# Shift's transfers issued by ACT, SP's loads and spills in another order, and every band applied by DVE

## The reference, cut to what matters

```
y = x + attention(layernorm(x)) @ W_proj + b_proj
out = y + moe(layernorm(y))

attention, per head (window m = 64, p = 8, four levels):
  A0[q] = q . k of the 64 keys that end at the query           (a band of 64 in a window of 128 keys)
  Al[q] = q . 8 pooled keys of the previous block, l = 1..4     (blocks of 64, 128, 256, 512 rows)
  mn = min over the five levels of max(A_level)
  weights = exp(A - mn), pooled ones times 8, 16, 32, 64; divided by their sum
  output = weights . values (and pooled values)

moe: 8 experts, softmax gate, the top 2 renormalised; expert e: (a * sigmoid(b)) @ Wo + bo, a and b the halves of y @ W1[e] + b1[e]
```

## Time and profile before

| | |
|---|---|
| runs | 333.83, 325.39, 331.42 us; median 331.42 |
| profiled execution | 322.26 us, of which the span of its instructions is 320.4 us |
| PE busy | 272.8 us, 85% of the span |
| DVE, ACT, POOL busy | 189.8, 159.8, 129.0 us |
| start, until unit 0's first score | 0 to 41.3 us |
| attention, eight units | 41.3 to 205.9 us |
| experts | 205.9 to 320.4 us |
| transfers | 28.35 MB |

### The profile page before, as it was taken

How to read it: one execution, slowest core, us unless ns; L and a number is a source line. 1 busy time by engine, 2 the same in 40 slices (tenths; PEclk the granted TensorE clock), 3 DMA queues, 4 the chain that set the end, 5 groups by cost and what they waited for, 6 DMA issues and landing times.

```text
span 320.4 us, 6664 instructions
## 1 busy us (share of the span) xinstructions
PE 272.8 (85%) x2382; PEld 225.5 (70%) x2382; DVE 189.8 (59%) x515; ACT 159.8 (50%) x325; POOL 129.0 (40%) x217
## 2 busy tenths in 40 slices
PE   7784588499798599937999796799999999999994
PEld 5563486487686589826787685577888877888883
DVE  7837428528436243520465638776787698777773
ACT  7574235135346336722429437464458654555551
POOL 7103203402000000110016238167788478888882
PEclk9796956859779579995989996999999999999999
DMA  8139843340569533145117355010000000000000
GB/s 219 29 119 332 283 112 74 92 93 1 170 255 267 130 74 110 21 102 154 28 30 231 77 186 177 5 27 8 8 11 9 9 10 8 18 10 8 16 10 16
DMA packets 25391, 28.35 MB, mean 88 GB/s; under 512 B 12976, under 2 KB 19248, under 8 KB 25360
## 3 DMA queue, kind: packets, MB, share of 16 engines
q1 hardware_dynamic: 25216, 27.55, 29.5%
q10 hardware_dynamic: 144, 0.39, 0.4%
HBM read 15.81 MB, written 8.91 MB: 77 GB/s over the span
## 4 chain that ended last, share of the span: by engine, by line
PE 60%; DVE 13%; DMA 8%; SPq 8%; ACT 6%; issue 4%; POOL 0%; DVEq 0%; ACTq 0%
PE bank L1102 11%; PE bank L1104 10%; PE bank L1103 10%; DMA qst<-nshiftT 7%; PE bank L1248 7%; PE bank L1218 7%; PE bank L1230 4%; SPq L459 4%; SPq L512 2%; PE bank L1205 2%; DVE work L1032 2%; PE bank L1156 2%; PE bank L1171 2%; DVE arena L1058 1%; PE bank L1251 1%
## 5 line engine op out<-in xcount | busy, mean ns | idle before, releaser
L710 POOL TENSOR_TENSOR work<-work 128x256 f32<-128x256 f32 x110 | 80.7, 738 | 27.1 <-DVE work L1085 14.5
L1085 DVE SCALAR_TENSOR_TENSOR work<-bank,comb,work 128x256 f32<-128x256 f32 x128 | 59.2, 481 | 24.8 <-ACT work L834 23.4
L834 ACT ACTIVATE work<-bank 128x256 f32<-128x256 f32 x128 | 48.3, 384 | 44.8 <-PE bank L1104 44.5
L653 POOL COPY vaug<-vwin 128x64 f32<-128x64 f32 x64 | 16.6, 305 | 94.5 <-PE bank L1251 86.3
L809 ACT ACTIVATE work<-bank 128x512 f32<-128x512 f32 x64 | 37.5, 595 | 32.9 <-PE bank L1230 32.6
L1032 DVE TENSOR_TENSOR work<-work,const 128x512 f32<-128x512 f32 x48 | 32.4, 688 | 31.5 <-ACT work L809 31.4
L1248 PE MATMUL bank<-work,vaug 128*36 128x64 f32 x1024 | 46.5, 240 | 4.9 <-DVE work L1032 4.8
L1248 PEld LDWEIGHTS bank<-work,vaug 128*36 128x36 f32 x1024 | 35.6, 125 | 14.8 <-DVE work L1032 5.9
L1218 PE MATMUL bank<-qst,pkm 104*128 104x64 f32 x128 | 23.5, 345 | 23.3 <-DMA qst<-nshiftT 23.3
L1218 PEld LDWEIGHTS bank<-qst,pkm 104*128 104x128 f32 x128 | 22.7, 270 | 24.9 <-issue 24.1
L1230 PE MATMUL bank<-qmk,kst 98*128 98x256 f32 x128 | 33.4, 350 | 0.0
(11 more groups left out here) (165 smaller groups left out, 472.7 us busy)
## 6 DMA issues: line engine op xcount, KB each, us to landing
w_stage<-w SPq DMA_DIRECT2D x6, 512.0 KB, 4.2
qst<-q_rows SPq DMA_DIRECT2D x7, 384.0 KB, 3.8
kst<-k_rows SPq DMA_DIRECT2D x7, 384.0 KB, 3.9
qmk<-q_rows SPq DMA_DIRECT2D x28, 96.0 KB
q_rows<-arena SPq DMA_DIRECT2D x2, 1024.0 KB, 5.2
k_rows<-arena SPq DMA_DIRECT2D x2, 1024.0 KB, 6.0
pkm<-p_rows SPq DMA_DIRECT2D x28, 48.0 KB
q_rows<-arena SPq DMA_DIRECT2D x2, 512.0 KB, 3.2
```

What stands on the lines that cost most here:

```text
L710: gp.tensor_tensor(gacc[t % 2][:, :], gacc[t % 2][:, :], gtmp[(adds - 1) % TMP_RING][:, :], ALU.add).then_inc(acc_done, 1)
L834: act.activation(sig[hn % SIG_RING][:, :], bank[hn % HID_BANKS][:, HID:2 * HID], ACT.Sigmoid).then_inc(sig_done, 1)
L1085: dve.scalar_tensor_tensor(dst[:, :], bank[hn % HID_BANKS][:, 0:HID], comb[:, t, e:e + 1], sig[hn % SIG_RING][:, :], ALU.mult, ALU.mult).t ...
```

## The change

1. **Shift's transfers by ACT.** `load_shift` leaves SP. A new step `shift load` follows three places behind the first guard; in it ACT waits for `nshiftT` and issues both transfers, `qst`'s first.
2. **Guards earlier.** `GUARD_AT` goes from [6, 4, 4, 4, 4, 4, 4] to [6, 2, 2, 2, 2, 2, 2].
3. **Start.** ACT's zeroing of `pkm[1]` moves ahead of `xT`; its zeroing of the two `vaug` and the head pattern of `pkm[1]` move from between `xT` and the keys to a new step `value blanks` behind `heads`, ahead of `v`. Two of the three transfers into `pks` are issued by ACT right behind the evacuation of `kp`.
4. **SP's order.** At the start the keys' and head queries' loads go ahead of the spills. In the loop the order is: keys and head queries of u+1; in unit 2 the spills of queries and pooled keys; queries and pooled keys of u+2; in unit 2 the spill of keys; gather_outputs(u-1). The first two loads of `w1` are now behind gather_outputs(5).
5. **Spilled keys** are written once (2 x 128 rows, 1 MB a batch instead of 1.5 MB) and read by two transfers instead of one.
6. **Bands.** `BARRED_BY_PE` is empty: 16 products less on PE, 16 minima more on DVE.
7. **POOL.** The bias is added to `xres` in units 1 and 2 (steps guard 2 and guard 3) instead of at 25.61 us and after apply (1, 1).
8. `IDLE` counts: 20 instead of 14 ahead of the first `xT`, 6 instead of 12 ahead of the first guard, 6 instead of 8 ahead of the first score.

```diff
-GUARD_AT = [6, 4, 4, 4, 4, 4, 4]
+GUARD_AT = [6, 2, 2, 2, 2, 2, 2]
-    s += [*[("heads", 0, j) for j in range(GH)], ("weight columns",), ("v", 0, 0), *[("guard", 0, m) for m in range(2)], ("shift", 0), ("shiftT", 0), ("second buffers",)]
+    s += [*[("heads", 0, j) for j in range(GH)], ("weight columns",), ("value blanks",), ("v", 0, 0), *[("guard", 0, m) for m in range(2)], ("shift", 0), ("shiftT", 0), ("shift load", 0), ("second buffers",)]
                 if i == first + 2:
                     s.append(("shiftT", u + 1))
+                if i == first + 3:
+                    s.append(("shift load", u + 1))
-BARRED_BY_PE = (2, 5)
-IDLE = {("xT", 0, 0): 14, ("xT", 0, 1): 2, ("kp", 0): 6, ("guard", 0, 0): 12, ("shiftT", 0): 4, ("score", 0, 0): 8}
+BARRED_BY_PE = ()
+IDLE = {("xT", 0, 0): 20, ("xT", 0, 1): 2, ("kp", 0): 6, ("guard", 0, 0): 6, ("shiftT", 0): 4, ("score", 0, 0): 6}
             def spill_keys(b):
                 wait_gen_done(sp, ("qk", b, 1, 1))
-                spill(k_dram[b][2 * P:SLOTS * P, :], k_hi, k_spilled[b])
-                spill(k_dram[b][0:2 * P, :].rearrange("(n p) t -> p n t", n=2), arena[:, 2:4, :], k_spilled[b])
+                spill(k_dram[b].rearrange("(n p) t -> p n t", n=2), arena[:, 2:4, :], k_spilled[b])
-                    for n, src in enumerate((kpool_hi, kpool_lo, kpool_hi)):
-                        move(pks[n * HR:(n + 1) * HR, :], src[g:P:NG, :]).then_inc(pks_in, 16)
+                    move(pks[HR:2 * HR, :], kpool_lo[0:P:NG, :]).then_inc(pks_in, 16)
-                sp.dma_start(kst[s][0:SR, PAD:].bitcast(F32), k_dram[b][g:SLOTS * P:NG, :]).then_inc(kst_in[s], 16)
+                sp.dma_start(kst[s][0:2 * HR, PAD:].bitcast(F32), k_dram[b][g:2 * P:NG, :]).then_inc(kst_in[s], 16)
+                sp.dma_start(kst[s][2 * HR:SR, PAD:].bitcast(F32), k_dram[b][g:P:NG, :]).then_inc(kst_in[s], 16)
             load_queries(0)
             load_pooled(0)
-            spill_queries(0)
             load_keys(0)
-            spill_pooled(0)
             load_head_queries(0)
+            spill_queries(0)
+            spill_pooled(0)
+            load_queries(1)
+            load_pooled(1)
             spill_keys(0)
-            load_queries(1)
             for u in range(UNITS):
-                load_shift(u)
-                if u == 0:
-                    load_pooled(1)
                 if u + 1 < UNITS:
                     load_keys(u + 1)
                     load_head_queries(u + 1)
-                if u >= 2 and u != NG + 1:
-                    gather_outputs(u - 2)
                 if u == NG - 2:
                     spill_queries(1)
                     spill_pooled(1)
-                    spill_keys(1)
-                if u == NG:
-                    gather_outputs(NG - 1)
                 elif u == NG + 1:
                     load_reciprocals(0)
                 if u + 2 < UNITS:
                     load_queries(u + 2)
                     load_pooled(u + 2)
+                if u == NG - 2:
+                    spill_keys(1)
+                if 0 < u < UNITS - 1:
+                    gather_outputs(u - 1)
                 if u + 2 == UNITS:
                     for i in range(STAGES - 1):
                         load_w1(i)
# ACT
+            act.activation(pkm[1][0:SR, :, :, :]..., zeros[...], ACT.Copy).then_inc(blank_act, 1)   # ahead of the schedule
+                elif kind == "shift load":
+                    u = step[1]
+                    wait_gen_done(act, ("shiftT", u))
+                    act.dma_start(qst[u % 2][SR:SR + 2 * GH, :].bitcast(F32), nshiftT[:, :].bitcast(F32)).then_inc(shift_in[u % 2], 16)
+                    act.dma_start(qmk[u % 2][SR:SR + 2, :, :].bitcast(F32), nshiftT[:, :].bitcast(F32)).then_inc(shift_in[u % 2], 16)
+                elif kind == "value blanks":
+                    shift_heads(1)
+                    for i in range(2):
+                        blank_values(i)
                     if b == 0:
-                        blank_values(1)
-                        shift_heads(1)
-                        act.activation(pkm[1][0:SR, :, :, :]..., zeros[...], ACT.Copy).then_inc(blank_act, 1)
+                        act.wait_ge(gen_hi, sum(s[0] in ACT_FIRST for s in GEN[:GEN_AT[step] + 1]))
+                        for n in (0, 2):
+                            act.dma_start(pks[n * HR:(n + 1) * HR, :].bitcast(F32), kpool_hi[0:P:NG, :].bitcast(F32)).then_inc(pks_in, 16)
```

More of the change, by code:

```diff
@@ L273, in build @@
         rden, stage = denom[0:H, :], denom[WIN:WIN + VC, :]
-        q_dram, k_dram = ([nc.dram_tensor(f"{n}_rows{b}", (SLOTS * P, T), F32).ap() for b in range(B)] for n in ("q", "k"))
+        q_dram = [nc.dram_tensor(f"q_rows{b}", (SLOTS * P, T), F32).ap() for b in range(B)]
+        k_dram = [nc.dram_tensor(f"k_rows{b}", (2 * P, T), F32).ap() for b in range(B)]
         p_dram = [nc.dram_tensor(f"p_rows{b}", (SLOTS * P, NB * LK), F32).ap() for b in range(B)]
@@ L437, in build @@
         PV_PARTS = [(ci, j) for ci in range(2) for j in range(GH)]
-        QST, KST, QMK, SHIFT, PKM = (qst_in, 3, 1), (kst_in, 3, 1), (qmk_in, 4, 4), (shift_in, 2, 2), (pkm_in, 0, 4)
+        QST, KST, QMK, SHIFT, PKM = (qst_in, 3, 1), (kst_in, 3, 2), (qmk_in, 4, 4), (shift_in, 2, 2), (pkm_in, 0, 4)
         block = ctx.enter_context(nc.Block())
@@ L507, in load_pooled @@
                 if u == 1:
-                    sp.wait_ge(blank_act, 4)
+                    sp.wait_ge(blank_act, 2)
                 else:
@@ L526, in load_keys @@
                     return
-                sp.wait_ge(k_spilled[b], 32)
-                sp.dma_start(kst[s][0:SR, PAD:].bitcast(F32), k_dram[b][g:SLOTS * P:NG, :]).then_inc(kst_in[s], 16)
+                sp.wait_ge(k_spilled[b], 16)
+                sp.dma_start(kst[s][0:2 * HR, PAD:].bitcast(F32), k_dram[b][g:2 * P:NG, :]).then_inc(kst_in[s], 16)
+                sp.dma_start(kst[s][2 * HR:SR, PAD:].bitcast(F32), k_dram[b][g:P:NG, :]).then_inc(kst_in[s], 16)
             def load_head_queries(u):
@@ L542, in load_head_queries @@
                         sp.dma_start(qmk[s][j:SR:GH, j, :].bitcast(F32), q_dram[b][GH * j + g:SLOTS * P:GH * NG, :]).then_inc(qmk_in[s], 16)
-            def load_shift(u):
-                s = u % 2
-                wait_gen_done(sp, ("shiftT", u))
-                move(qmk[s][SR:SR + 2, :, :], nshiftT[:, :]).then_inc(shift_in[s], 16)
-                move(qst[s][SR:SR + 2 * GH, :], nshiftT[:, :]).then_inc(shift_in[s], 16)
             def gather_outputs(u):
@@ L568, in _ @@
             load_pooled(0)
+            load_keys(0)
+            load_head_queries(0)
             spill_queries(0)
-            load_keys(0)
             spill_pooled(0)
-            load_head_queries(0)
+            load_queries(1)
+            load_pooled(1)
             spill_keys(0)
-            load_queries(1)
             for u in range(UNITS):
-                load_shift(u)
-                if u == 0:
-                    load_pooled(1)
                 if u + 1 < UNITS:
@@ L670, in _ @@
             for i in range(2):
-                gp.wait_ge(blank_act, 2 + i)
+                gp.wait_ge(blank_act, 3 + i)
                 for j in range(GH):
@@ L675, in _ @@
             then(gp.memset(vwin[0:WIN, 0, :], 0.0))
-            wait_gen_done(gp, ("qk", 0, 1, 1))
-            add_bproj(0)
             values_of(0)
@@ L696, in _ @@
                     n_ln += 1
-                elif step == ("apply", 1, 1):
+                elif step == ("guard", 2, 0):
+                    add_bproj(0)
+                elif step == ("guard", 3, 0):
                     add_bproj(1)
@@ L730, in _ @@
             shift_heads(0)
+            act.activation(pkm[1][0:SR, :, :, :].rearrange("p c j k -> p (c j k)"), zeros[0:SR, 0:1].broadcast_to([SR, NB * GH * LK]),
+                           ACT.Copy).then_inc(blank_act, 1)
             sc = lo = hn = 0
@@ L739, in _ @@
                     act.activation(xT_hi[:, PAD + 512 * n:PAD + 512 * (n + 1)], gen_bank(step)[:, :], ACT.Copy).then_inc(gen_hi, 1)
-                    if step == ("xT", 0, 1):
-                        blank_values(0)
                 elif kind == "qk":
@@ L745, in _ @@
                     if b:
-                        act.wait_ge((q_spilled, k_spilled)[t][0], 32)
+                        act.wait_ge((q_spilled, k_spilled)[t][0], (32, 16)[t])
                         wait_unit_loads(act, 0, (QST, KST)[t])
@@ L757, in _ @@
                     if b == 0:
-                        blank_values(1)
-                        shift_heads(1)
-                        act.activation(pkm[1][0:SR, :, :, :].rearrange("p c j k -> p (c j k)"), zeros[0:SR, 0:1].broadcast_to([SR, NB * GH * LK]),
-                                       ACT.Copy).then_inc(blank_act, 1)
+                        act.wait_ge(gen_hi, sum(s[0] in ACT_FIRST for s in GEN[:GEN_AT[step] + 1]))
+                        for n in (0, 2):
```

(3 more changed lines are left out.)

## The result

Four runs of the changed kernel took 301.18, 303.64, 306.36 and 305.37 us, median 304.5; beside them four runs of the kernel before (the three of above and one of 322.48 us) have a median of 328.4 us. The ratio is 0.9366, with a 95% interval of 0.9183 to 0.9549; it compares only the faster runs of each kernel, 301.18, 303.64 and 305.37 us with 322.48 and 325.39, so it is not the quotient of the medians. The forecast was 299 us, with a range of 287 to 317. The profiled execution took 301.18 us, its span 299.0; the sum had given 291.3 us for one like it.

A forecast was written before the change was run, and what follows sets the result against it. Bound by PE's products and its 23.3 us of waits for the shift's transfer, with low clock behind waits. Terms sum to -31.0 on 322.3, giving 291.3 us, times 1.028 = 299 us; range 287 to 317.

The forecast's parts named there:

- Waits: PE's waits for the shift ahead of units 2, 3, 5, 7 and inside unit 6 go: -16.8 us.
- Start: Before unit 0, earlier heads and ACT issuing the first shift bring the first pooled scores sooner: -5.0 us.
- Ahead of unit 1: The wait there stays, as its guard is still at i = 6, and `qmk`'s part leaves 0.6 us later: +0.6.
- rival A: Shift transfers fly longer, so waits and low clock remain in attention: 317 us, chance 0.18.
- Clock: Three low-clock stretches behind waits of units 2, 3 and 5 return to full clock, worth half their length: -11.2 us.
- Bands: Fourteen band products leave PE's path, -4.6 us; the added DVE minima cost +1.4 us in unit 7.
- Weights of the experts: First `w1` loads, queued behind gather_outputs(5), arrive about 2.5 us into unit 7: +1.0 us, between 0 and 4.
- ACT and DVE tight: Allowance for fuller ACT and DVE: +1.4 us in unit 6, 0.55 in each of units 2 to 5, +2.2.
- Loads: SP's issues are covered and unit 4's pooled keys land before its guard: zero, with 0.7 us in hand.
- Rival B: PE waits at the early guards for pooled keys, most likely in units 3 and 4: 310 us, chance 0.11.
- C: Rival: ACT reaches the shift's issue no sooner than SP's queue did, so the waits stay: 325 us, chance 0.07.
- D: Rival: many short waits inside units keep the clock at 0.5 through whole units: 347 us, slower, chance 0.04.

The follow-up runs named there:

- first: Kernel before with the guards of units 2 to 7 at i = 2 instead of 4, SP still issuing the shift; ratio 0.998.
- second experiment: Kernel before with the shift's two transfers issued by ACT, guards at their old places; ratio 0.9892.
- fifth experiments: Changed kernel with the guards of units 2 to 7 back at i = 4, ACT still issuing; median 320.26 us, ratio 0.98.
- quiet flight: Changed kernel in which SP waits for unit 1's shift to land before issuing keys and head queries of unit 2; one run, 303.03 us.
- fourth experiments: Changed kernel with the bands of k = 2 and 5 by PE's product again; median 303.27 us, ratio 0.9331.

## Why the prediction was right, and where not

Direction, size and the main mechanism held: the queue's delay and the waits went. Against the profiled executions the sum said -31.0 and -21.1 were measured, 9.9 us off. By one of the forecast's own signs it was wrong, too: attention was to take no more than 145 us and took 146.8. The clock's term is why.

- **Waits, -16.8.** Right: 14.66 us of waits ahead of units 2, 3, 5 and 7 became 0.35, and unit 6's 2.17 became 0.16. The two parts are needed together, as the first, second and fifth experiments show. I had them as one term and never said what either would do alone. The 3.5 us of flight in it was too short for unit 2, where `qmk`'s part left at 92.08 and PE went on at 97.01, 4.9 us later; the cover was nearly used up there.
- **Start, -5.0.** Measured -4.1. The first shift was copied at about 31 us, as worked out; `qmk`'s part left at 32.27, where I had 31.9, and flew 4.9 us, near the longer of my two (5.1 and 3.5).
- **Ahead of unit 1, +0.6.** Measured +1.6. I gave the second transfer the flight time of unit 1 before, 3.6 us, though the change puts SP's loads for unit 2 right beside it: rival A's mechanism, at a place where I had not applied it. The quiet flight shows it, 3.1 against 5.8 us.
- **Clock, -11.2.** This is the term that was mis-sized. Of the three stretches that I removed those of units 2 and 5 went; unit 3 kept one of 6.6 us, behind idle times of 0.35 and 0.42, and its mean clock is 0.79 where it was 0.77. Units 0 and 1 had mean clocks of 0.55 and 0.69, where they had 0.66 and 0.80, which comes to some 11 us more at the lower level. From the units' lengths I put the excess at 1.5, 2.5 and 3.4 us (an estimate: each unit's measured length less its length before and its own terms); together 7.4 of the 9.9 us. The step "a wait brings a low stretch, no wait brings none" failed in its second half. The trace of before could have told it. I counted four low stretches in attention, and it has more: 13 us of unit 0, 194.0 to 200.8 in unit 7, and one in unit 5 with no idle time just ahead of it. There PE had been busy for 13.76 of 13.76 us, the last 6.7 of them at the full clock, when the clock fell:

```profile
146.04:159.80 13.76, 13.76 (x140) 10.83 (x140) 4.08 (x8) 5.17 (x9) 0.77 (x4) 0.75 0.30 77
159.90:163.10 3.20, 3.20 (x18) 2.84 (x20) 1.92 (x4) 0.25 (x2) 0.00 (x0) 0.50 0.00 0
```

  I had also read unit 5's first stretch as 7.6 us, and it is 7.0, and the 8.3 us that the best end takes for units 0 and 1 stand on no row.
- **Bands, -4.6 and +1.4.** The traces say -4.5 and +1.8, and the time says nothing either way.
- **Weights of the experts, +1.0 with the minima's +1.4.** Unit 7 grew by 5.1 us. Of that 2.5 to 2.9 are the two late loads (from the two experiments that issue them early; unit 6 got some 1 us longer there), at which I had reckoned 1.0 (upper end 4): ACT reached the weights 6.1 us into the unit instead of 3.1 (185.62 before, its unit 7 began at 182.48), and each load behind them waited too. The rest is the minima, and a clock of 0.62.
- **ACT and DVE tight, +1.4 and +2.2.** Hardly seen: unit 6 took 12.8 us where 13.8 were allowed, and unit 4 13.2 where 13.6 were (an estimate: its 21.1 us less 7.38 of wait and 0.64 of bands, and the 0.55).
- **Loads, 0.** Right: from unit 1 on PE never waited for a guard's pooled keys. Rival B did not happen.
- **Rivals.** A happened ahead of unit 1, and by 0.35 us ahead of unit 3. Its rule from the Trainium skill, "DMA: Bandwidth & Descriptors", section "Issuing engines are not separate DMA queues", that transfers of different issuers interleave on the same engines, agrees with the quiet flight. That another issuer saves only the time to initiate agrees with the small gain of the second experiment (1.1%) in size, though not in kind: ahead of unit 5 the wait fell by 5.85 us, more than the 1.3 of the two issues, and the waits ahead of units 2 and 3 are what was left. C did not: ACT issued within 0.15 us of each copy. Of D's mechanism, short waits with a low clock behind them, unit 3 is a small case.
- **From the execution to the runs.** I scaled by 1.028. The changed kernel's median lies 1.011 above its profiled execution; scaling the measured 301.2 by 1.028 would have given 309.6. This error ran against the 9.9 us, and took 5 of them back: that 299 was so near 304.5 is in part luck.

What stays open: what brings and holds the low clock in unit 0, and in unit 3 behind idle times under 1 us. In unit 0 it was there in every version, for 10 us (the second and fourth experiments) up to the whole unit, and it was not traced to a cause.

## What to carry to other kernels

- A transfer that waits behind others' issues on an in-order queue, and a transfer that is asked for too late, are two causes with one symptom. Moving the issuer without moving the producer gave 1%, moving the producer alone gave nothing, and the whole change, which has both, gave 6%, and 2% with the producer put back; so cost the pair, and look for the next place with the same pattern: here one number more, unit 1's guard, gave another 14.5 us.
- When an issue is moved, list what the other queues send in the same microseconds; the flight of a small transfer nearly doubled beside six loads, and whether it leaves ahead of them or behind may count as much as how many they are.
- When PE is nearly free of waits its clock becomes the largest unknown. Put a range on it instead of counting each old low stretch as won.

## What the runs showed of the hardware

- The granted clock fell to 0.5 behind idle times of 1.84 us (PE filled up to it), 1.88 and, in unit 3 of the changed kernel, behind 0.35 and 0.42 us with PE busy for nearly all of the time around them. In unit 5 before it fell with no idle time at all, after 13.76 us of 13.76 busy, and was at 0.50 for 3.4 us. It stayed at 1.00 behind 2.17 us in unit 6 before.
- In unit 1 of the changed kernel PE was busy for 12.1 of 12.1 us (60.7 to 72.8) with the clock at 0.50; unit 2, which follows, ran its 15.5 us at 1.00.
- The shift's second transfer, 32 KB, took 3.1 us from issue to PE with none of SP's transfers beside it, 5.8 beside six loads, 6.4 beside the spills, and 7.9 in the second experiment, with the DMA engines busy for 0.99 of that time.
